# Moving projections, feed-forward pieces and filler matmuls between the slots of a transformer kernel's hand-written schedule

## The reference, cut to what matters

```python
x = x + tanh(g_xattn[0]) * xattn0(layernorm(x), ctx, ...)
x = x + tanh(g_ffn[0])   * moe_top2(layernorm(x), router_w, router_b, expert_weights)
x = x + tanh(g_xattn[1]) * xattn1(layernorm(x), ctx, ...)
h = gelu(quant(layernorm(x)) @ quant(w1).T)      # 1024 wide
x = x + tanh(g_ffn[1])   * (quant(h) @ quant(w2).T)
```

## Time and profile before

| | |
|---|---|
| median of three runs | 733.78 us (733.73 to 738.92) |
| profiled execution, its own time | 736.02 us |
| its span, first to last instruction | 734.2 us |
| mean granted TensorE clock | 0.974 |
| PE / DVE / ACT / POOL busy, share of span | 93 / 75 / 57 / 22 % |

### The profile page before, as it was taken

The page is one execution under the profiler, slowest core; times in us unless marked ns, Lnnn a source line. Parts: engine busy times, 40 slices in busy tenths (PEclk is TensorE's granted clock), DMA queues, the critical chain, the costliest instruction groups (busy, mean ns, idle before and its releaser), DMA issues.

```text
span 734.2 us, 10157 instructions
## 1 busy us (share of the span) xinstructions
PE 681.7 (93%) x3616; PEld 331.5 (45%) x3616; DVE 549.8 (75%) x1201; ACT 418.5 (57%) x538; POOL 163.3 (22%) x243
## 2 busy tenths in 40 slices
PE   5999999999999999999999999999999999998867
PEld 2433333454545545454554545543444344442345
DVE  2678997876888778887788877878597859893174
ACT  3336766854345733546435563376777577666655
POOL 6213334531002320122201321024210310130032
PEclk9988999989999999999999999999999999999889
DMA  7985588314210241113403133122522152200001
GB/s 240 271 251 179 187 250 269 80 45 131 43 45 30 47 128 44 46 41 94 107 6 74 45 86 88 29 90 87 129 59 61 45 129 52 52 9 9 0 8 51
DMA packets 39026, 66.74 MB, mean 91 GB/s; under 512 B 5184, under 2 KB 13888, under 8 KB 38720
## 3 DMA queue, kind: packets, MB, share of 16 engines
q1 hardware_dynamic: 38128, 65.57, 31.9%
q10 hardware_dynamic: 848, 0.53, 0.2%
HBM read 38.29 MB, written 27.26 MB: 89 GB/s over the span
## 4 chain that ended last, share of the span: by engine, by line
PE 69%; DVE 15%; ACT 8%; issue 4%; DMA 3%; POOL 0%; SPq 0%; DVEq 0%; ACTq 0%
PE psO L846 13%; PE psS L818 11%; PE psX L769 7%; PE psT L832 7%; DVE mx L1301 5%; PE psX L907 5%; PE psX L883 4%; PE psX L908 4%; PE psX L909 4%; ACT pt L1087 3%; PE psX L789 3%; PE psX L959 2%; PE psX L863 2%; DVE xs L1448 2%; PE psX L802 2%
## 5 line engine op out<-in xcount | busy, mean ns | idle before, releaser
L1087 ACT ACTIVATE pt<-psT 128x1024 f32<-128x1024 f32 x256 | 262.1, 1024 | 210.0 <-PE psT L832 207.4
L1301 DVE TENSOR_REDUCE mx<-psS 128x1 f32<-128x512 f32 x512 | 325.8, 680 | 52.6 <-PE psS L818 52.3
L818 PE MATMUL psS<-ks,qs 48*128 48x512 f32 x512 | 142.4, 504 | 2.2 <-DVE mx L1301 1.8
L846 PE MATMUL psO<-pt,vg 128*32 128x512 f32 x1024 | 140.5, 621 | 0.1
L832 PE MATMUL psT<-qs,ks 50*128 50x512 f32 x512 | 115.6, 422 | 9.1 <-ACT pt L1087 7.5
L818 PEld LDWEIGHTS psS<-ks,qs 48*128 48x128 f32 x512 | 55.9, 186 | 133.7 <-issue 76.3
L1448 DVE SCALAR_TENSOR_TENSOR xs<-psX,coef,xs 128x256 f32<-128x256 f32 x128 | 61.8, 483 | 35.6 <-PE psX L909 32.3
L832 PEld LDWEIGHTS psT<-qs,ks 50*128 50x128 f32 x512 | 52.4, 190 | 26.1 <-ACT pt L1087 22.0
L619 POOL TENSOR_TENSOR parts<-qf,parts 128x512 fp32r<-128x512 f32 x30 | 38.5, 1284 | 113.5 <-ACT parts L1031 113.5
L638 POOL TENSOR_SCALAR lnw<-mv 128x4 f32<-128x4 f32 x14 | 3.2, 228 | 265.7 <-DVE mv L1191 265.7
L907 PE MATMUL psX<-moeh,xh 128*128 128x512 f32 x128 | 57.1, 446 | 1.7 <-DVE xs L1448 1.7
(11 more groups left out here) (139 smaller groups left out, 779.2 us busy)
## 6 DMA issues: line engine op xcount, KB each, us to landing
ks<-kd SPq DMA_DIRECT2D x64, 192.0 KB, 4.0
qs<-qd SPq DMA_DIRECT2D x64, 192.0 KB, 4.6
kd<-parts SPq DMA_DIRECT2D x16, 512.0 KB, 2.9
qd<-parts SPq DMA_DIRECT2D x16, 512.0 KB, 2.7
kd<-parts SPq DMA_DIRECT2D x16, 256.0 KB, 3.5
qd<-parts SPq DMA_DIRECT2D x16, 256.0 KB, 3.4
ctxb<-in_ctxT SPq DMA_DIRECT2D x7, 512.0 KB, 4.1
xs<-in_x SPq DMA_DIRECT2D x4, 512.0 KB, 6.0
```

What stands on the lines that cost most here:

```text
L818: mm(psS[:, i % 3, :], qs[at:at + KR, 2 * g + a, k * P:(k + 1) * P], ks[at:at + KR, 2 * g + a, :], start=True, stop=True).then_inc(pe_s, 1)
L846: i = mm(psO[32 * j:32 * j + 32, :], vg[:, p % 2, k, g * GH + j, :], pt[:, s % RING, j, :], start=k == 0, stop=k == NT - 1, tile_position= ...
L1087: a(pt[:, G % RING, 2 * half:2 * half + 2, :], psT[:], ACT.Exp, scale=SCALE).then_inc(a_exp, 1)
L1301: v.tensor_reduce(mx[:, w // GH % 2, r, col:col + 1], psS[:, i % 3, :], AX.X, ALU.max).then_inc(v_max, 1)
```

## The change

- Start: sample 1's four first-layer projections K(1,0), K(1,1), Q(1,0), Q(1,1) leave the prologue and the lead and are put into slots 0, 2, 4 and 6 of period 0 (Q0, K0, Q1, K1). Both XT of sample 1 stand in the prologue, ahead of the first S. The lead has a WARM in each of its slots 20 to 34, where it had twelve. The FILL of slots 4 and 6 become one in slot 5.
- Period 5: tiles of sample 0 follow the table LATER in place of the formula; tile 3's HT and F2 land in slots 14 and 15 of period 6. The FILL of period 6 in slots 14 and 15 are gone.
- Period 7: five more FILL, in slots 22, 24, 26, 28 and 30.
- Tail: a FILL of eight matmuls ahead of the first XB of sample 3; the second XB (tokens of tiles 2 and 3) moves ahead of the transposes of sample 2's tile 2, HQ(0) with it; HQ(1) and HQ(2) of sample 3 move ahead of the F2 of sample 2's tiles 2 and 3.

```diff
+LATER = ((17, 20, 22, 24), (21, 24, 28, 30), (26, 30, 32, 34), (32, 46, 46, 47))
...
     lead = -1
-    put(lead, 20, ("XT", (1,)))
     put(lead, 21, ("RELOAD", (0, 2)))
-    put(lead, 22, ("RELOAD", (0, 3)), ("SPLIT", ("K", 1, 1)))
-    put(lead, 25, ("SPLIT", ("Q", 1, 0)))
-    put(lead, 28, ("SPLIT", ("Q", 1, 1)))
+    put(lead, 22, ("RELOAD", (0, 3)))
...
-    put(0, 0, ("LD", ("x3",)))
+    put(0, 0, ("SPLIT", ("Q", 1, 0)), ("LD", ("x3",)))
+    put(0, 2, ("SPLIT", ("K", 1, 0)))
+    put(0, 6, ("SPLIT", ("K", 1, 1)))
...
-    put(0, 4, ("LD", ("k1",)))
+    put(0, 4, ("SPLIT", ("Q", 1, 1)), ("LD", ("k1",)))
...
-            for t, (hq, h0, h1, f) in enumerate(LATE if p == NP - 2 else ()):
+            for t, (hq, h0, h1, f) in enumerate(LATE if p == NP - 2 else LATER if p == NP - 3 else ()):
...
-            for t in range(NT if p < NP - 2 else 0):
+            for t in range(0):
...
-    for s in (20, 21, 23, 24, 26, 27, 29, 30, 31, 32, 33, 34):
+    for s in range(20, 35):
         put(lead, s, ("WARM", (2,)))
-    put(0, 4, ("FILL", (2, 0)))
-    put(0, 6, ("FILL", (2, 0)))
+    put(0, 5, ("FILL", (2, 0)))
...
-        for s in (13,) if p <= B else (15, 18) if p == B + 1 else (14, 15, 18) if p == B + 2 else (15, 18):
+        for s in (13,) if p <= B else (15, 18) if p == B + 1 else (18,) if p == B + 2 else (15, 18, 22, 24, 26, 28, 30):
             put(p, s, ("FILL", (3 if s == 18 else 2, 1)))
...
-    put(NP, 4, ("XB", (0, NC, 0, 2)), ("HQ", (2,)), last[0], away[0], ("LND", (b, 2, 4)), ("LNN", (0, b, 2, 4)), ("F1", (0,)))
-    put(NP, 5, ("HQ", (3,)), *rows[1], ("XQ", (2, 4)), ("F1", (1,)), last[1], away[1], *rows[2], ("XB", (0, NC, 2, 4)))
-    put(NP, 5, ("HQ", (0,)), last[2], away[2], ("F1", (2,)), ("HQ", (1,)), *rows[3], ("F1", (3,)), last[3], away[3])
-    put(NP, 6, ("HQ", (2,)), ("HQ", (3,)))
+    put(NP, 4, ("FILL", (8, 1)), ("XB", (0, NC, 0, 2)), ("HQ", (2,)), last[0], away[0], ("LND", (b, 2, 4)), ("LNN", (0, b, 2, 4)), ("F1", (0,)))
+    put(NP, 5, ("HQ", (3,)), *rows[1], ("XQ", (2, 4)), ("F1", (1,)), last[1], away[1], ("XB", (0, NC, 2, 4)), ("HQ", (0,)))
+    put(NP, 5, *rows[2], ("F1", (2,)), ("HQ", (1,)), last[2], away[2], *rows[3], ("F1", (3,)), ("HQ", (2,)), last[3], away[3])
+    put(NP, 6, ("HQ", (3,)))
...
-    out += [("SPLIT", ("K", 1, 0)), ("WARM", (5,)), ("XT", (0,))]
+    out += [("WARM", (5,))] + [("XT", (c,)) for c in range(NC)]
```

## The result

The changed kernel takes 733.46 us, the kernel before 737.38 us (medians of 20 executions each, taken together; the three executions known before the prediction had 733.78). The ratio is 0.9956 with an interval of 0.9938 to 0.9974: 3.2 us faster (1.9 to 4.6), where 7.8 us were forecast. The ratio leaves out the few executions over 1.5% above the fastest of their kernel, so it is not quite that of the medians. The profiled execution took 735.24 us against 736.02, its span is 733.4 against 734.2.

What follows compares the result with a forecast made beforehand. PE was taken as the bound, busy 681.7 of 734.2 us, with the chain mostly through it. Terms -2.4 - 1.3 - 1.1 - 1.5 + 0 - 1.5 = -7.8 took the median 733.78 to 726.0 us, range 719.5 to 733.

Steps and rivals of the forecast that it cites:

- The start, -2.4: Prologue to slot 8: first T at 42.5, T of slot 8 at 62.6 instead of 64.96, 2.4 us gained.
- rival "slower": Start: store and reload traffic holds the `qs<-mt` transfer, first T no earlier; +6.7 instead of -2.4, 735.1 us; chance 0.07.
- the lower bound: Start at its best: eight slots take 18.9 instead of 20.1 us and T comes another 0.4 earlier, -4.0 us.
- The price of four projections: Slots 0 to 7 of period 0: with four projections, eight slots at full clock take 20.1 us.
- Spread of LATER, -1.3: Period 5: spreading gelu-tile work over later slots, as LATE does in period 6, gains 1.3 us.
- The two FILLs, -1.1: Period 6, slots 14 and 15: both removed FILLs are on the chain at 0.54 us each, gaining 1.1 us.
- Period 7, -1.5: End of period 7: new FILLs hide in PE's waits and the clock holds, gaining 1.5 us.
- The tail, 0 and -1.5: Tail: FILL of eight worth 0 (bounds -0.9 and +2.2); earlier XB and HQ gain 1.5 us (bounds 0 and -2.5).
- fillers fail: Period 7 and tail: clock falls all the same, reordered tail gains only 0.4 us; 728.6 us; chance 0.15.
- a price of 1.7 us: Period 6, slots 14 and 15: transposes replacing FILLs could let the clock fall, costing up to 1.7 us.

Runs made afterwards that it cites:

- s_later: The kernel before with LATER for period 5 and without the FILLs in slots 14 and 15 of period 6, alone; ratio 0.9985.
- a_no_start: The changed kernel with the start of the kernel before; ratio to the kernel before 0.9954.
- f7_no_1415: The kernel before with the five FILLs of period 7 and without the FILLs in slots 14 and 15 of period 6; ratio 0.9934.
- a_no_tail: The changed kernel with the tail of the kernel before; ratio to the kernel before 0.9946.
- s_start: The kernel before with the changes of the start alone; ratio 0.9999.
- s_tail: The kernel before with the changes of the tail alone (FILL of eight, XB and HQ earlier); ratio 1.0006.
- s_fill7: The kernel before with the five FILLs of period 7 alone; ratio 0.9919.
- a_fill5: The changed kernel with two more FILLs in period 5, in slots 22 and 27; ratio to the kernel before 0.9919.
- a_no_fill8: a_fill5 without the FILL of eight in the tail, reordering kept; ratio to the kernel before 0.9922.
- a_no_later: The changed kernel with period 5 back on the formula and the FILLs in slots 14 and 15 of period 6 back; ratio to the kernel before 0.9924.
- best_b: a_no_start with two FILLs in slots 22 and 27 of period 5 and the last WARM before the first T six matmuls long; ratio to the kernel before 0.9910.

## Why the prediction was wrong

The sign was right, the size was not (-3.2 us, forecast -7.8), and the median, 733.46, lies above the range, 719.5 to 733. Of the 7.5 us between it and the forecast of 726.0, 3.6 come from the base: three executions had a median of 733.78, twenty have 737.38. The rest is the change. The step that failed outright is the spread of LATER: it was to give 1.3 us and gives none, and it brings a low clock in a place where the prediction had none. The start and the tail were to give 3.9 us together and give nothing in the mean; the end of period 7 gave more than was said and hides a part of this. By the prediction's own terms:

- **The start, -2.4.** T0 was put at 42.5 and came at 43.59: I had only the first eight of the S pairs and the transfer in the sum, and T also stands behind the S of slots -4 to 0, which DVE paces. The transfer was no limit (the rival "slower" falls with it). The 0.4 us that the lower bound added from a figure of the Trainium skill, "DMA: Bandwidth & Descriptors", section "Anatomy of one DMA", no run isolates; that section describes DMAs issued by GpSimd, and this one is SP's. The price of four projections, 20.1 us for eight slots, was right (20.38). That leaves -1.0 against the profile of before, and in the mean of 14 profiles 0. The failed step is the comparison with one trace, in which the clock was low for 10.3 us behind T0; the same code without that takes 14.7 us for these slots (s_later, a_no_start), so the four projections cost 5.7 us there and not 3.1.
- **Spread of LATER, -1.3.** The work of PE is only moved: T176 to T192 falls from 41.54 to 39.65 us (a_no_start, the one profile with LATER that has neither a dip nor more FILLs), T192 to T208 rises from 33.42 to 35.65 once the two FILLs are taken out of the comparison (f7_no_1415). That is +0.3. The 1.3 us came from comparing the stretch XB to XB of period 5 with that of period 6, and LATE puts an F2 of period 6 into slot 52, behind the next XB: it runs at 668.96, 0.87 us on the chain, and is not in the 69.88 us. The remaining 0.4 us stay open.
- **The two FILLs, -1.1.** Measured 0.5. One of the two was on the chain; the earlier trace rows show only that one, and I counted both.
- **What LATER brought.** The clock falls in period 5. I had a fall there for another reason, transposes in the place of FILLs in slots 14 and 15, where the Trainium skill, "TensorE: Matmul & The Clock Gate", Part 4, speaks against the trade; that place stayed at 1.00 in every profile with LATER. It fell in slots 28 to 31, where PE had short waits for DVE. The cost in the changed kernel's profile is 3.0 us (42.69 against 39.65 to T192), but in the mean of the four profiles with LATER and without more FILLs 1.5 us, since one has no dip and two a shorter one. In the ratios the three kernels that have LATER and the five FILLs of period 7, but no more FILLs in period 5 (the changed one, a_no_start, a_no_tail), are at 0.9946 to 0.9956, the seven others with those five FILLs at 0.9910 to 0.9934. The means are 0.003 apart, 2.2 us; single intervals overlap.
- **Period 7, -1.5.** The mechanism was right, the term too small. In the two profiles of before and after T244 to T255 falls from 20.02 to 17.87 us, but the profile of before had one of the short falls there. Of the four profiles without these FILLs two have the clock low for 20 to 24 us (s_start, s_tail), one for 6.8, one not at all; of the ten with them none. The ratio of s_fill7 alone is 0.9919, 6.0 us (4.1 to 7.7). From T244 to the end these four profiles take 67.2 us in the mean and the ten 63.5, so 3.7 us of it can be located; where the rest lies no profile shows.
- **The tail, 0 and -1.5.** In the changed kernel's profile -1.0, in all ratios nothing. The early XB did come 1.4 us sooner after the F2, and HQ(2) ahead of the accumulation. HQ(3) even came at 722.3, as forecast. But the last tiles then wait for each other through the two psX banks (F2, accumulation, transposes, eviction), which my sum passed over: from HQ(3) to the end it is 11.1 us, where it was 9.8. And PE's wait of 2.97 us ahead of the F2 of tile 1, that was 1.27 at low clock, is followed by a fall of the clock in five of the seven profiles with this FILL. The FILL ahead of the first XB only moves the low stretch.

The measured parts can be added up in two ways. By ratios: 0 for the start, -0.2 for LATER and its FILLs at full clock, -6.0 for period 7, 0 for the tail, +2.2 for the fall in period 5, together -4.0. By the means of the profiles: 0, -0.2, -3.7, 0 and +1.5, together -2.4. The measured -3.2 lies between. The shares of period 7 and of the fall in period 5 are thus known to a few us only. Of the rivals, "fillers fail" was wrong in mechanism; the one that would have been needed, a list that unloads PE so that the clock falls, was named for a wrong place and only with a price of 1.7 us.

No candidate is measurably ahead of s_fill7, which is one line of the change: a_fill5, a_no_fill8, a_no_later and best_b lie between 0.9910 and 0.9924 with intervals of 0.003.

## What to carry to other kernels

Where many executions differ by more than the change, read the clock of each before its trace, and take no term, and no base either, from few executions; here two of the six terms, the start and period 7, were set by where one execution's low stretch happened to lie. A schedule that moves work off a full TensorE gives nothing back by itself, and can cost time through the clock in the slots that it empties; a few filler matmuls in slots where TensorE waits anyway were nearly free here, and with them it held. When two stretches are compared to price a schedule, check that each holds all of its own work.

## What was not expected of the hardware

- At the end of period 7 the same code at the same load ran at half clock for 0, 6.8, 20.5 or 23.9 us. PE was busy 2.19 of 3.40 us ahead of the fall of 23.9 us; in s_later, where the clock held, it was busy 2.07 to 2.16 of 3.40 us in three such stretches. With one FILL of two matmuls, 0.6 us, in every second slot it never fell in ten profiles.
- A fall needed no long wait: ahead of 548.6 us in the changed kernel the longest piece of idle PE that the timeline names is 0.94 us. The Trainium skill, "TensorE: Matmul & The Clock Gate", section "A second HAM failure mode", describes falls from frequent short idle pieces, and these rows agree.
- In a_no_fill8 the clock stayed at half for 10.3 us although PE was busy in all of them, with S pairs, WARMs and a projection; the kernel before does the same from 48.5 us.
- Within 4 us behind the 16 router matmuls of 8 columns (L895 in the kernel before) the clock fell in 36 of their 56 places in the fourteen profiles. PE was busy all of the 3.40 us ahead of the fall at 335.2 in the kernel before, for one.
